# A four-layer kernel on one core: the split x kept once in DRAM, loaded by four 32-row transfers a step, with two reorderings and the recurrence written out

## The reference

```python
xr, gate = jnp.split(x @ W_in.T, 2, axis=-1)          # 512 -> 2 x 1024
xc = silu(causal_conv4(xr + t_emb) + b_conv)
xn = layernorm(xc) * ln_g + ln_b
Bm, Cm, dt = jnp.split(xn @ W_xproj.T, 3, axis=-1)    # 16 states
Ad = 1.0 + tanh(dt @ W_dt.T + b_dt) * 0.01 * A
Bd = Bm * jnp.minimum(norm(xn), 1.0)
def step(h, inputs):                                  # 128 steps in sequence
    h = jnp.clip(h * ad[:, :, None] + bd[:, :, None] * xt[:, None, :], -10.0, 10.0)
    return h, jnp.einsum('bd,bdh->bh', ct, h)
return (ys + D * xn) * silu(gate) @ W_out.T
```

## Time and profile before

| quantity | value |
|---|---|
| time, median of 3 runs | 3843.36 us (3834.58 to 3845.87) |
| time of the profiled execution | 3847.87 us |
| its span, first to last instruction | 3846.1 us |
| tensor engine busy | 3471.1 us (90%) |
| VectorE busy | 2965.7 us (77%) |
| DMA traffic | 631.06 MB, mean 164 GB/s |
| state updates of layer 0's recurrence | 538.7 to 1192 us |
| state updates of layer 3's recurrence | 3168.0 to 3829 us |

### The profile page before, as it was taken

How to read it: one execution, slowest core, us unless ns; L and a number is a source line. 1 busy time by engine, 2 the same in 40 slices (tenths; PEclk the granted TensorE clock), 3 DMA queues, 4 the chain that set the end, 5 groups by cost and what they waited for, 6 DMA issues and landing times. The chain is left out here.

```text
span 3846.1 us, 63520 instructions
## 1 busy us (share of the span) xinstructions
PE 3471.1 (90%) x22068; PEld 2250.8 (59%) x22068; DVE 2965.7 (77%) x3172; ACT 1345.1 (35%) x2078; POOL 1855.8 (48%) x1384
## 2 busy tenths in 40 slices
PE   7999839999996899999999999997999938999998
PEld 6777614444444667777777777765777723444444
DVE  4766769999995777777777777753566759999998
ACT  3555511222122444334444444332455522112121
POOL 2555646555553124444444444342455555555554
PEclk9999969999997899999999999998999978999999
DMA  3566675555553233222322222223466675555553
GB/s 126 216 249 251 255 245 213 200 203 213 207 203 124 86 107 108 75 78 80 113 83 91 83 81 72 72 75 117 173 252 238 229 289 193 216 196 203 203 204 142
DMA packets 288590, 631.06 MB, mean 164 GB/s; under 512 B 33472, under 2 KB 35904, under 8 KB 288224
## 3 DMA queue, kind: packets, MB, share of 16 engines
q1 hardware_dynamic: 281200, 615.49, 45.3%
q10 hardware_dynamic: 7104, 11.81, 0.8%
HBM read 390.75 MB, written 241.70 MB: 164 GB/s over the span
## 5 line engine op out<-in xcount | busy, mean ns | idle before, releaser
L1201 DVE CUSTOM_DVE_ANT_0 l3r_g<-l3r_g,l3r_pv,l3r_cf 128x1024 f32<-128x1024 f32 x512 | 642.4, 1341 | 31.6 <-PE l3r_pv L1010 23.7
L1201 DVE CUSTOM_DVE_ANT_0 l0r_g<-l0r_g,l0r_pv,l0r_cf 128x1024 f32<-128x1024 f32 x512 | 642.1, 1340 | 23.6 <-PE l0r_pv L1010 15.5
L142 PE MATMUL l1h_ps_p<-l1h_xh,l1c_wh 128*128 128x512 f32 x768 | 322.3, 420 | 5.6 <-issue 3.5
L144 PE MATMUL l1h_ps_p<-l1h_xl,l1c_wh 128*128 128x512 f32 x768 | 308.3, 401 | 0.0
L2187 POOL TENSOR_TENSOR l1h_st<-l1h_veps 128x1 f32<-128x1 f32 x64 | 35.3, 552 | 561.8 <-DVE l1h_veps L2045 561.8
L143 PE MATMUL l1h_ps_p<-l1h_xh,l1c_wl 128*128 128x512 f32 x768 | 305.3, 397 | 0.0
L1799 ACT ACTIVATE l1h_pt<-l1h_ps_t 128x512 f32<-128x512 f32 x256 | 151.0, 590 | 369.8 <-PE l1h_ps_t L1672 369.8
L1025 PE MATMUL l3r_py<-l3r_g,l3r_cd 128*32 128x512 f32 x2048 | 254.5, 613 | 0.8 <-issue 0.8
L1025 PE MATMUL l0r_py<-l0r_g,l0r_cd 128*32 128x512 f32 x2048 | 253.2, 613 | 1.2 <-ACT l0r_y L1110 1.2
L2085 DVE TENSOR_TENSOR l1h_e<-l1h_e,l1h_mx 128x1024 f32<-128x1024 f32 x128 | 216.4, 1691 | 4.4
L2104 DVE TENSOR_TENSOR l1h_vt<-l1h_ps_p,l1c_dc 128x512 f32<-128x512 f32 x64 | 44.2, 691 | 220.0 <-PE l1h_ps_p L144 220.0
(11 more groups left out here) (400 smaller groups left out, 8963.1 us busy)
## 6 DMA issues: line engine op xcount, KB each, us to landing
l0r_x<-xhl_s SPq DMA_DIRECT2D x128, 512.0 KB, 5.5
l3r_x<-xhl_s SPq DMA_DIRECT2D x128, 512.0 KB, 5.6
xhl_s<-l0a_xo SPq DMA_DIRECT2D x116, 512.0 KB, 4.6
xhl_s<-l3a_xo SPq DMA_DIRECT2D x116, 512.0 KB, 4.6
gate_s<-l0a_gate SPq DMA_DIRECT2D x64, 256.0 KB, 2.6
l0r_dx<-dx_s SPq DMA_DIRECT2D x32, 512.0 KB, 7.8
l0r_gate<-gate_s SPq DMA_DIRECT2D x32, 512.0 KB, 8.6
l0r_crow<-feed_s SPq DMA_DIRECT2D x64, 256.0 KB
```

The costliest lines, as they stand in the source:

```text
L142: pe.matmul(out, wh, xh, start=first, stop=False)
L144: return pe.matmul(out, wh, xl, start=False, stop=last)
L1201: dve._custom_dve(bass.dve_ops.TENSOR_ADD_SAT, out=g[:, t, j, :], in0=g[:, (t - 1) % TS, j, :], in1=pv[(k.off + t + j) % 3][:, :], s0=cf[: ...
```

## The change

Five edits are made together.

1. `xhl` has 64 rows for a position instead of 128: each row is stored once, so a batch takes two stores of 512 KB instead of four.
2. `load_x` issues, for each t, four loads of 32 partitions instead of one of 128. Each reads 16 DRAM rows, as a leading dimension of 2 with stride zero over them. The semaphore `x_ld` is waited on at 64 instead of 16.
3. `turn(n)` in the projection stands after `project_x(T, it)` of odd `it` instead of after `project_gate(T, it)` of even `it`.
4. In attention `values(g, 0)` moves behind `mix_w` to stand next to `values(g, 1)`, and `values(g, 2)` next to `values(g, 3)`.
5. `rounds` is written out over all 32 blocks; and at the start of the recurrence `load_x(1, 1)` is issued after the coefficient loads instead of before.

```diff
@@ rounds
-    for k in range(HEAD):
-        body(Turn(0, k))
-    with eng.Fori(0, (NBLK - 2 * HEAD) // ROUND) as i:
-        for r in range(ROUND):
-            body(Turn(i, HEAD + r))
-    for k in range(NBLK - HEAD, NBLK):
+    for k in range(NBLK):
         body(Turn(0, k))
@@ project_phase, SP
-        x_v = dram["xhl"].rearrange("s (h a c l b) (p i) -> s c l h a b p i", h=2, a=2, c=2, l=2, p=2)
+        x_v = dram["xhl"].rearrange("s (h a l b) (p i) -> s l h a b p i", h=2, a=2, l=2, p=2)
...
-                for c in range(2):
-                    for l in range(2):
-                        sp.dma_start(x_v[:, c, l, :, n // GB % 2, n % GB, n // GB // 2, :],
-                                     xo[:, r, l, :].bitcast(F32).rearrange("s (h i) -> s h i", h=2)).then_inc(xo_st[r], 16)
+                for l in range(2):
+                    sp.dma_start(x_v[:, l, :, n // GB % 2, n % GB, n // GB // 2, :],
+                                 xo[:, r, l, :].bitcast(F32).rearrange("s (h i) -> s h i", h=2)).then_inc(xo_st[r], 16)
@@ project_phase, tensor engine
                     project_x(T, it)
+                    if it % 2 == 1:
+                        turn(TB * (T - 1) + it // 2)
                     if rows and it == KI - 1:
                         turn_x(T + 1, TB - 1)
                     project_gate(T, it)
-                    if it % 2 == 0:
-                        turn(TB * (T - 1) + it // 2)
@@ recurrence_phase, SP
             def load_x(k, q):
                 at_least(sp, bmm, GJ * TS * (k - 1))
                 for t in range(TS):
-                    sp.dma_start(x[:, q, t, :, :].bitcast(F32).rearrange("p c i -> p (c i)"),
-                                 dram["xhl"][bass.ds(k * TS + t, 1), :, :].rearrange("t p i -> (t p) i")).then_inc(x_ld[TS * q + t], 16)
+                    for r in range(4):
+                        sp.dma_start(x[r * 32:(r + 1) * 32, q, t, :, :].bitcast(F32).rearrange("p c i -> p (c i)"),
+                                     dram["xhl"][bass.ds(k * TS + t, 1), r * 2 * GB:(r + 1) * 2 * GB, :].to_broadcast([2, 2 * GB, DI]))\
+                            .then_inc(x_ld[TS * q + t], 16)
...
                         load_x(0, 0)
-                        load_x(1, 1)
                         load_tokens(0, 0)
                         store_feed()
                         load_feed(0, 0)
                         load_feed(1, 1)
+                        load_x(1, 1)
@@ recurrence_phase, tensor engine
-                    pe.wait_ge(x_ld[TS * k.parity() + t], 16 * k.uses())
+                    pe.wait_ge(x_ld[TS * k.parity() + t], 64 * k.uses())
@@ attend_phase, tensor engine
-                values(g, 0)
                 turn(g, 1)
...
+                values(g, 0)
                 values(g, 1)
                 turn(g, 2)
...
-                values(g, 2)
                 turn(g, 3)
...
+                values(g, 2)
                 values(g, 3)
```

More of the change, by code:

```diff
@@ L518, in store_high @@
                 act.wait_ge(xoh, n + 1)
-                for c in range(2):
-                    act.dma_start(x_v[:, c, 0, :, n // GB % 2, n % GB, n // GB // 2, :],
-                                  split_rows(n)[:, 0, :].bitcast(F32).rearrange("s (h i) -> s h i", h=2)).then_inc(xo_st[n % 2], 16)
+                act.dma_start(x_v[:, 0, :, n // GB % 2, n % GB, n // GB // 2, :],
+                              split_rows(n)[:, 0, :].bitcast(F32).rearrange("s (h i) -> s h i", h=2)).then_inc(xo_st[n % 2], 16)
             def halves(n):
@@ L526, in halves @@
                 if n < B - 2:
-                    at_least(act, xo_st[r], 64 * (n // 2))
+                    at_least(act, xo_st[r], 32 * (n // 2))
                 else:
@@ L595, in _ @@
             act.wait_ge(xol, B)
-            for c in range(2):
-                act.dma_start(x_v[:, c, 1, :, n // GB % 2, n % GB, n // GB // 2, :],
-                              split_rows(n)[:, 1, :].bitcast(F32).rearrange("s (h i) -> s h i", h=2)).then_inc(xo_st[n % 2], 16)
+            act.dma_start(x_v[:, 1, :, n // GB % 2, n % GB, n // GB // 2, :],
+                          split_rows(n)[:, 1, :].bitcast(F32).rearrange("s (h i) -> s h i", h=2)).then_inc(xo_st[n % 2], 16)
             act.wait_ge(dxm, B)
@@ L842, in _ @@
                 sp.wait_ge(g_st[r], 16 * NT * KI // 2)
-                sp.wait_ge(xo_st[r], 64 * B // 2)
+                sp.wait_ge(xo_st[r], 32 * B // 2)
                 sp.wait_ge(dx_st[r], 16 * B // 2)
@@ L917, in _ @@
             for r in range(2):
-                pool.wait_ge(sent[1][r], 64 * B // 2)
+                pool.wait_ge(sent[1][r], 32 * B // 2)
             pool.memset(cd[:, :, :, :, :], 0.0).then_inc(zeroed, 1)
@@ L2254, in scratch @@
         return nc.dram_tensor(name, shape, dt, kind="Internal").ap()
-    dram = dict(gate=scratch("gate_s", (PAIR * NBLK, GJ, TS // PAIR, GB, DI)), xhl=scratch("xhl_s", (S, P, DI)),
+    dram = dict(gate=scratch("gate_s", (PAIR * NBLK, GJ, TS // PAIR, GB, DI)), xhl=scratch("xhl_s", (S, P // 2, DI)),
                 dx=scratch("dx_s", (PAIR * NBLK, GJ, TS // PAIR, GB, DI)), feed=scratch("feed_s", (2, 2, S, 2 * P)),
```

2 lines of the change are left out of this document (1 added, 1 removed).

## The result

| | before | after |
|---|---|---|
| median (range, runs) | 3841.15 us (3834.58 to 3845.87, 4 runs beside the changed kernel) | 5761.01 us (5752.10 to 5763.71, 4 runs) |
| ratio, 95% interval | | 1.500 [1.497, 1.503] |
| span of the profiled execution | 3846.1 us | 5761.6 us |
| projection, layers 0 and 3 | 498.1, 510.8 | 478.7, 489.7 |
| recurrence, layers 0 and 3 | 711.3, 720.8 | 1708.2, 1710.3 |

The kernel takes half as long again. The phases are cut at the barriers: one begins with its first instruction behind a barrier in the trace. The sum is -19.4 + 996.9 - 30.4 - 21.1 + 989.5 = 1915.5 us: both recurrences lost nearly 1000 us each, and the other three phases gained 71.

A forecast was written before the change was run, and what follows sets the result against it. Two DMA engines carrying x were to bound the recurrence, where VectorE did before. 3847.9 + 1890 (recurrences) - 10 (stores) - 14 (turn) - 18 (values) = 5696, given as 5695 us; range 5470 to 6155.

The forecast's parts named there:

- mechanism (a): Recurrence: each x load's outermost dimension of 2 puts x on two DMA engines; 5695 us, chance 0.90.
- The period: Recurrence: a block takes 50.1 us of ring time (x 41.1, coefficients 5.1, other traffic 3.9) against VectorE's 20.05.
- SP's added issues: Recurrence: 16 x loads a block instead of 4 cost SP 8 to 10 us, hidden in its waiting.
- The stop halfway through a block: Recurrence: dx and gate land behind the next block's x, so gating, turns and later updates wait; period stays 50.1 us.
- rival (c): Recurrence: the ring runs empty between blocks, 10 to 15 us on top of 50; 6560 us, chance 0.03.
- The start: Recurrence start: x(0) issued at 508.5 takes 41.1 us; stores and coefficients of two blocks follow, until 565.8.
- x(1) behind the coefficients: Recurrence start: issuing the second block's x after the coefficients spares the first block another 41 us.
- The loops: Recurrence written out: gaps around the rounds worth 19.5 us if VectorE is the bound, 0 here.
- Stores once: Projection end: half the bytes shorten ScalarE's wait for a store, 5 us a layer, bounds 0 and 8; -10.
- `turn` later: Projection: tensor engine's waits for a tile's last piece shrink, 7 us a layer, bounds 5 and 10; -14.
- `values` together: Attention: fewer changes of matmul kind, 128 times 0.14 us; -18 us, bounds 0 and -24.
- Rival (b): Recurrence: x still spreads over the engines, fits under 20.05 us from eight on; 3786 us, chance 0.06.

The follow-up runs named there:

- e4: e3 with each x load's 32 different rows in two runs of 16 far apart, outermost dimension 2 with a real stride: 5785.02 us, one run.
- e2: Changed kernel, 64 stored rows, but copies adjacent: one x load a step, repetition inside; coefficients by four loads with 16 outermost: 3746.84 us.
- e3: e1 with each step's x in four loads of 32 different rows instead of one load: 3846.83 us, one run.
- e5: Changed kernel, each x load repeating 8 rows four times instead of 16 rows twice (other data, for time only): 4503.54 us, one run.
- e1: Changed kernel with edits 1 and 2 undone: 128 stored rows, one 128-row x load a step: 3776.53 us, ratio 0.983.
- e8: e3 with the coefficients by eight loads of 16 partitions, 16 outermost, instead of two with 4: 3766.13 us.
- e10: Changed kernel with the second block's x issued before the coefficients again: 5765.22 us.
- e11: e2 with the second block's x issued before the coefficients again: 3740.95 us, ratio 0.974.
- e7: e2 with the recurrence's loop put back (four blocks, four rounds of six, four blocks): 3768.64 us.
- e9: e3 run again unedited, timed: 3822.56 us, from 3792.44 to 3840.66.

## Why the prediction was right, point by point

5761.0 us against 5695 forecast, 1.2% above it, by mechanism (a).

- **Two engines, and why.** Right. Share 0.13 and 52 GB/s; e4 rules out the zero stride, e2 the second reading, e3 against e4 the partitions, and e5 places four outermost at 102 GB/s. Over the recurrence the share was 0.23 at 80 GB/s, not the forecast's 0.17 to 0.2. The Trainium skill, "DMA: Bandwidth & Descriptors", section "Why a DMA increments its semaphore by 16 and not by 1", takes the largest number up to 16 that divides the outermost dimension of both sides. The traces agree: 0.13 by 2, 0.26 by 4, 0.48 by 8, and bursts of 1.01 by 64 (e2) or 128 (before).
- **The period.** Right in form, 1.6 to 1.7 us too small: 51.7 and 51.8 against 50.1. At 26 GB/s an engine the bytes alone are 50.1 x 25.5 / 26 = 49 us, so some 2.6 us a block aren't bytes. Over 29 blocks a layer the excess is 96 us, as much as the two recurrences exceed the forecast by (+1986 instead of +1890). The term that the sum lacks is, as I read it, a price for each load; no run takes it apart from what loads cost each other where they meet. From e1 and e3 it is estimated: share 0.75 - 0.59 of 20.05 us, for 12 more loads, is 3.2 / 12 = 0.27 us of each engine. Added to the forecast's sums it gives 53.3, 32.8 and 22.5 us for two, four and eight outermost; the means are 51.7, 32.1 and 22.3. It is of the right size, and too large for two by 1.6; its make-up was not resolved. It is no fixed price either: e8 has six loads more a block than e3 and a share of 0.76 in the same stretch.
- **SP's added issues: 0.** Right for the time, wrong in the reason. The term was 8 to 10 us a block, hidden; SP in fact spends 37.28 us on the x of a block. That costs nothing only because the ring is what it waits for.
- **The stop halfway through a block.** Right: dx lands 19.0 us after its issue (median), `turns` waits for both gatings, the tensor engine's clock is 0.50 meanwhile, and the ring doesn't run dry (rival (c)): in the block shown the share is 0.12 or more in every microsecond.
- **The start.** The duration was right, the moment not. From the issue of x(0) to the first update are 541.84 - 481.06 = 60.8 us, near the forecast's 60. But x(0) was issued at 481.06, 27 us earlier than before and not at 508.5: 19 for the shorter projection, and 8 more since the stores it waits for land sooner. In e1, with the stores whole, x(0) is issued 10.4 us into the phase as before; in e2, with half of them, after 2.3. In layer 3 these 8 us are 9. So the 96 us of excess are 96 from the blocks' periods, -17 from these two starts, and 17, or 8.5 a layer, that are left for the loads of the first three blocks and the end, not taken apart.
- **x(1) behind the coefficients.** It was to spare the first block 41 us; e10 shows that it does, and that the end gains 0 to 4. The sum had not credited it, but the text let it look useful. With full-width loads it costs some 6 us a layer (e11), by way of the output weights that stand behind it.
- **The loops: 0 here, 19.5 if VectorE is the bound.** 0 was right. In e7 the recurrences show 11.4 and the total 21.8.
- **Stores once: -10.** Right: e2 against e1, projection alone, -5.4 and -3.1.
- **`turn` later: -14.** Out of its bounds of 5 and 10 a layer: e1 has -12.6 and -17.9. The forecast saw the wait for the last piece; its answer after the change is `PE l0a_ptr L413 <- ACT l0a_xc L498: 1.3, 1, 1.3`, 9.0 less instead of 7. Missed were other waits of `turn`, at the end of layer 0's projection (from 440 us on): for `xn`, 4.7 us before and 0.7 after. Missed too was a new one: the tensor engine waits for `l0a_pad` 9.8 us in all instead of 5.8. Over all its waits in the projection the tensor engine gained 10 us in layer 0 and 12 in layer 3 (before against e1); the other 2 and 6 us of the phases are open.
- **`values` together: -18, bound -24.** Out of its bounds: -30.4, and -30.1 in e1. The step that failed is the reading of the earlier trace rows, which has one kind of group only. The tensor engine's timeline in the kernel after, around a doubled group and around a transpose that now stands alone:

```profile
2800.53 0.40 PE L139 MATMUL l1h_ps_p<-l1c_wl,l1h_oh 128*128 128x512 f32 x1
2800.86 0.64 PE L1675 MATMUL l1h_ps_o<-l1h_pt,l1h_v 128*32 128x128 f32 x16
2801.43 0.66 PE L1665 MATMUL l1h_ps_t<-l1h_ident,l1h_e 128*128 128x128 f32 x4
2801.85 0.48 PE L137 MATMUL l1h_ps_p<-l1h_xh,l1c_wh 128*128 128x512 f32 x1
...
2804.51 0.39 PE L139 MATMUL l1h_ps_p<-l1h_xl,l1c_wh 128*128 128x512 f32 x1
2804.74 0.60 PE L1665 MATMUL l1h_ps_t<-l1h_ident,l1h_e 128*128 128x128 f32 x4
2805.09 0.48 PE L137 MATMUL l1h_ps_p<-l1h_xh,l1c_wh 128*128 128x512 f32 x1
```

A transpose behind a large matmul starts at the stream's step of 0.23 us and lasts 0.35 until the next large one. Here only the small products took 0.33 to enter, and transposes behind them 0.41 to leave. A pair of groups took 2 x (0.33 + 0.35 + 0.41) = 2.18 us and takes 1.90 (0.33 + 0.57 + 0.42 and 0.23 + 0.35); with 128 pairs 36 us, 30 measured. That is 0.24 a pair, not 0.14.
- **The sum** came out well partly by luck: +96 us on the recurrences, -16.5 on the projections and -12.4 on attention leave 67 us.
- **Rival (b), on the other side.** Its mechanism (16 engines) is e2 and e8: 3747 and 3766, against the 3786 given for it. Its threshold "fits from e = 8" is wrong: at eight, the kernel is slower than before by 56 us (one run).

## What to carry to other kernels

Before a load is split or made to repeat rows, look at the outermost dimension of its source: with 2, 4 and 8 there, so many of the 16 engines worked here. A share of DMA that stands at 2/16 or 4/16 while loads are outstanding is a narrow load, however low the page's mean looks. Put a repetition inside ([64][2, stride 0]) instead of outside ([2, stride 0][16]): the same bytes and the same saved stores, 3747 instead of 5761 us here. Judge a move at the start of a phase by what the end waits for: 42 us at the start were worth nothing where a ring was the bound. Ask, too, what else stands behind the transfer that is moved: x(1) behind the coefficients made nobody wait for x, but held up the output weights, and through ScalarE cost some 6 us a layer.

## What the runs showed of the hardware

- A load's price beyond its bytes: cutting 512 KB loads into four raised the DMA share from 0.59 to 0.75 at 210 GB/s. It doesn't show in the time while engines have room (e8), and e9, with the coefficients on four of them, has runs that scatter over 48 us.
- Loads already issued hold up the queue that issues more: SP's loads of x took 2.2 us each (median; up to 5.25), against 0.33 in e1, though the first eight took 0.61 to 0.81.

```profile
L856 SPq DMA_DIRECT2D l0r_x<-xhl_s x512: 612/2193/5250, 481.1 to 2129.1; - x171
```

```profile
L859 SPq DMA_DIRECT2D l0r_x<-xhl_s x128: 332/334/1471, 495.9 to 1136.7; - x128
```

These are the instructions of the x load's line, in after and in e1: duration in ns, least, median and most. Wide loads wait behind the narrow ones: dx landed 19.0 us after its issue instead of 7.8 before.
